# A block kernel on one core: the setup phase of the constants merged into the first attention phase

## The chip, the cores and the metric

The kernel runs on one core of a Trainium2 chip. The metric is the device time of one launch in microseconds (us), lower is better. The core has five engines that run their own instruction streams and meet at semaphores: TensorE (PE in the profile; its weight loads are PEld), VectorE (DVE), ScalarE (ACT), GpSimd (POOL) and SyncE (SP), which here only issues transfers. The granted clock of TensorE is on one of two levels, 1.2 or 2.4 GHz, and stands in the profile as a share of full speed (0.50 or 1.00). SBUF is the core's working memory of 128 partitions, PSUM (`ps`) the accumulators of TensorE.

## What is computed

Four layers on a residual stream `x` of 128 batches x 64 rows x 128 columns: cross attention, a chosen-token expert layer, a self and cross attention block with its own feed-forward part, and a mixture of experts. The outer function of the reference, and the projection part of the first layer, with which the kernel begins:

```python
    x = x + _L0_xattn_ref(_layernorm(x, axis=-1), ctx_1024, L0_xattn_Wq, ...)
    x = x + _L0_ffn_ref(_layernorm(x, axis=-1), L0_ffn_Wr, L0_ffn_Wqkv, L0_ffn_Wo)
    x = x + _L1_xattn_ref(_layernorm(x, axis=-1), ctx_1024, mask_SxS2_ik0, mask_Bx1x1xS2_if1, ...)
    x = x + _L1_ffn_ref(_layernorm(x, axis=-1), L1_ffn_router_w, ...)
...
    def _L0_xattn_ref(x, context, Wq, bq, Wk, bk, Wv, bv, Wo, bo):
        q = x @ Wq.T + bq
        k = context @ Wk.T + bk
        v = context @ Wv.T + bv
        ...
        scores = jnp.einsum('bhtd,bhcd->bhtc', q, k) / jnp.sqrt(jnp.asarray(d, x.dtype))
        attn = jax.nn.softmax(scores, axis=-1)
        out = jnp.einsum('bhtc,bhcd->bhtd', attn, v)
        ...
        return out @ Wo.T + bo
```

All of it is float32 with 16 heads of 8 columns. The mask `mask_SxS2_ik0` (64 x 64, int32) is used by the self attention of the third layer alone.

## The kernel before

The kernel is written as phases that follow one another: `setup_phase`, `attention_phase` 0 (first layer), `choice_phase` (second layer), `attention_phase` 1 and 2, `relu_phase` and `experts_phase`. Each phase is one block: the engines leave the one before through a barrier, its semaphores are cleared (`Signals.__exit__`, L56 and L57), and a jump leads into the code of the next one. Nothing of a phase starts before that.

**Constants.** All weights and small constants but the experts' lie in one array `pack` of 128 partitions x 5073 float32 (20,292 bytes a partition, 2536.5 KB). The table `COLS` gives each its columns, in the order a0, a1, a2 (643 columns for each attention phase: four weight matrices, the bias row of the output, three bias columns), ident, headmask, and the rest.

**`setup_phase` (L1926 to L1983)** loads `pack` in one transfer (L1943) and the self-attention mask in four (L1945, tile `qmi`). VectorE sets four small constants at once (L1958 to L1961), waits for `pack`, and makes from it the key biases by head group of the three attention phases (`bkm`, L1965), the scaled query bias of phase 0 (`bqs`, L1968) and a bf16 identity (`identb`, L1969). Then it waits for the mask and makes from it `qmask` and, by way of `qany`, `qdiag` and two matmuls of TensorE (L1952), `qscale` (L1971 to L1983). `bkm[1]`, `bkm[2]`, `identb`, `qmask` and `qscale` are read in attention phases 1 and 2 only.

**`attention_phase`, a = 0.** 16 groups of 512 rows. Group g+1 is prepared while the scores of group g are worked on (`pipelined`: `prep(0)`, `step(0)`, a loop of 14 steps, a last step). The preparation runs in four rounds through one PSUM bank, each a TensorE part and a copy out of PSUM by ScalarE:

- k: TensorE multiplies the context tile `ctxT` by wk (L539), ScalarE spreads it by head group into `kblk` (four ACTIVATEs, L305)
- xT: ScalarE applies the norm to `x_res` (L293), TensorE transposes (L535), ScalarE copies (L299)
- q: matmul (L541), copy (L312); v: matmuls (L544), copies (L319)

In front of xT stands the norm: statistics on VectorE (L391 to L400), `rstd` and `nmr` on GpSimd (L227, L230). A step has eight units `v`: scores (L574), maximum and shift on VectorE (L429, L431), transposes (L592), exponential on ScalarE (L338), product with v (L608); beside them run the pieces of the next group, and the end of the one before (`divide` L439 and L441, transposes L617, projection L626, residual L452).

At the phase's start SyncE issues in this order: `x_res` and `ctxT` of group 0, the same of group 1, and then two weights of the next phase, `wqkv` (1536 KB) and `woe` (512 KB); the loads of group g+2 follow when TensorE has finished the v round of group g. VectorE first fills `vblk` (L512, 128 x 4096 float32, and the two small L514 and L515), then comes to the statistics. ScalarE waits for `vblk`, and then for the first matmul.

## Time and profile before

| | us |
|---|---|
| median of 3 runs (2248.8 to 2259.13) | 2253.85 |
| the profiled execution, its own time | 2246.64 |
| span of its trace | 2244.8 |
| PE / DVE / ACT / POOL busy | 2005.9 / 1696.5 / 1060.5 / 518.5 |
| mean granted clock of TensorE | 0.959 |
| first instruction of attention phase 0 (a transfer) | 14.16 |
| first matmul of attention phase 0 | 17.70 |
| first score matmul, step 0 | 32.23 |
| end of the last instruction of attention phase 0 | 345.36 |

The 1.84 us between the span and the time lie outside the trace and are the same for both kernels here. The columns of the trace views: a timeline row is start, duration, engine, line, operation, tiles (out<-in), shape, how many were merged, and in brackets how long the engine had been idle and what ended that. PE matmuls of float32 are recorded as several passes, so one matmul of the code is two rows or more. SPq rows are transfers being issued, not landing.

### The profile page before, as it was taken

How to read it: one execution, taken by the hardware profiler on the slowest of the kernel's cores; microseconds unless marked ns; L12 is line 12 of the kernel's file. 1: busy time of each engine (PE TensorE's matmuls, PEld its weight loads, DVE VectorE, ACT ScalarE, POOL GpSimd, SP SyncE). 2: the span in 40 equal slices, each digit the busy share in tenths (PEclk: the TensorE clock that was granted, in tenths of full speed). 3: DMA queues.
4: the chain of work that ended last, by engine and by line, in shares of the span. 5: the costliest groups of instructions: out<-in, count | busy, mean ns of one | idle time of the engine just before them, and what ended most of it. 6: DMA issues, size and time to landing. Idle time of an engine off the chain costs nothing. (4 is left out here: it accounts for less than half of the span.)

```text
span 2244.8 us, 53059 instructions
## 1 busy us (share of the span) xinstructions
PE 2005.9 (89%) x19268; PEld 1549.8 (69%) x19268; DVE 1696.5 (76%) x4490; ACT 1060.5 (47%) x2084; POOL 518.5 (23%) x536
## 2 busy tenths in 40 slices
PE   5999995687769999996999997976999999999998
PEld 3666664566646666664666665755888888888887
DVE  4777775777736888885888885666888888888886
ACT  3666653455444555553555553433444444444443
POOL 1111110000001223221222222653322322232231
PEclk9999997999978999997999998997999999999999
DMA  3000000000000000001100001000000000000000
GB/s 123 29 19 27 28 10 1 1 1 0 0 1 2 0 0 0 0 0 29 30 28 28 28 10 64 0 0 1 6 11 5 5 5 10 5 5 10 5 5 10
DMA packets 27248, 30.41 MB, mean 14 GB/s; under 512 B 1936, under 2 KB 20624, under 8 KB 26896
## 3 DMA queue, kind: packets, MB, share of 16 engines
q1 hardware_dynamic: 27152, 29.28, 4.2%
q8 instruction: 42, 0.69, 0.1%
q14 instruction: 54, 0.44, 0.1%
HBM read 25.08 MB, written 4.19 MB: 13 GB/s over the span
## 5 line engine op out<-in xcount | busy, mean ns | idle before, releaser
L429 DVE TENSOR_REDUCE mx<-ps 128x8 f32<-128x512 f32 x384 | 261.9, 682 | 170.3 <-PE ps L574 169.9
L338 ACT ACTIVATE ex<-ps 128x512 f32<-128x512 f32 x384 | 230.1, 599 | 265.0 <-PE ps L592 263.2
L1111 ACT ACTIVATE moe_sg<-ps 128x512 f32<-128x512 f32 x288 | 172.5, 599 | 365.2 <-PE ps L1163 365.0
L1147 PEld LDWEIGHTS ps<-down,moe_act 128*128 128x128 f32 x2048 | 266.0, 191 | 33.0 <-DVE moe_acc L1340 12.6
L592 PE MATMUL ps<-pack,sh 128*128 128x128 f32 x1536 | 249.4, 285 | 32.1 <-DVE sh L431 31.5
L1147 PE MATMUL ps<-down,moe_act 128*128 128x128 f32 x2048 | 271.4, 275 | 5.8 <-DVE moe_acc L1340 5.8
L431 DVE TENSOR_TENSOR sh<-ps,mx 128x512 f32<-128x512 f32 x384 | 265.4, 691 | 13.2
L608 PEld LDWEIGHTS ps<-vblk,ex 128*64 128x64 f32 x6144 | 212.5, 139 | 64.6 <-issue 64.4
L608 PE MATMUL ps<-vblk,ex 128*64 128x32 f32 x6144 | 255.3, 226 | 0.0
L592 PEld LDWEIGHTS ps<-pack,sh 128*128 128x128 f32 x1536 | 168.2, 142 | 125.3 <-issue 65.2
L1322 DVE TENSOR_TENSOR moe_act<-ps,moe_sg 128x512 f32<-128x512 f32 x288 | 197.3, 685 | 68.2 <-PE ps L1163 55.6
L1340 DVE SCALAR_TENSOR_TENSOR moe_acc<-ps,moe_comb,moe_acc 128x128 f32<-128x128 f32 x768 | 215.4, 342 | 20.7 <-PE ps L1147 14.2
L574 PE MATMUL ps<-kblk,qd 32*64 32x256 f32 x3072 | 207.3, 386 | 1.5 <-issue 1.4
L1161 PE MATMUL ps<-moe_x_lo,moe_gate_hi 128*128 128x512 f32 x288 | 137.3, 477 | 26.0 <-DVE moe_act L1322 24.5
L305 ACT ACTIVATE kblk<-ps,bkm,pack 128x512 f32<-128x512 f32 x192 | 138.7, 782 | 39.2 <-PE ps L539 26.0
L574 PEld LDWEIGHTS ps<-kblk,qd 32*64 32x64 f32 x3072 | 108.5, 134 | 53.6 <-issue 8.9
L1038 POOL TENSOR_TENSOR moe_part<-moe_part 128x512 f32<-128x512 f32 x48 | 62.1, 1294 | 254.0 <-ACT moe_part L1104 254.0
L1163 PE MATMUL ps<-moe_x_hi,moe_gate_hi 128*128 128x512 f32 x288 | 114.3, 397 | 0.0
L1161 PE MATMUL ps<-moe_x_lo,moe_up_hi 128*128 128x512 f32 x288 | 114.2, 396 | 0.0
L1162 PE MATMUL ps<-moe_x_hi,moe_gate_lo 128*128 128x512 f32 x288 | 113.8, 395 | 0.0
L1163 PE MATMUL ps<-moe_x_hi,moe_up_hi 128*128 128x512 f32 x288 | 113.6, 395 | 0.0
L1162 PE MATMUL ps<-moe_x_hi,moe_up_lo 128*128 128x512 f32 x288 | 112.5, 391 | 0.0
(234 smaller groups left out, 3529.3 us busy)
## 6 DMA issues: line engine op xcount, KB each, us to landing
ctxT<-in_ctx SPq DMA_DIRECT2D x32, 256.0 KB, 2.8
x_res<-in_x SPq DMA_DIRECT2D x16, 256.0 KB, 2.9
kmi<-in_key_mask SPq DMA_DIRECT2D x16, 256.0 KB, 3.4
out<-moe_acc SPq DMA_DIRECT2D x16, 256.0 KB, 2.3
pack<-in_pack SPq DMA_DIRECT2D x1, 2536.5 KB, 9.4
wqkv<-in_wqkv SPq DMA_DIRECT2D x1, 1536.0 KB, 8.3
gate<-in_gate SPq DMA_DIRECT2D x6, 192.0 KB, 4.0
up<-in_up SPq DMA_DIRECT2D x6, 192.0 KB, 4.1
```

The costliest lines, as they stand in the source:

```text
L338: nc.scalar.activation(ex[:, u % 2], UB[u % 4].rearrange("p (c n) -> p c n", n=P), ACT.Exp).then_inc(e_ready, 1)
L429: nc.vector.tensor_reduce(mx[:, u % 2], sc, AX.X, ALU.max).then_inc(max_done, 1)
L431: nc.vector.tensor_tensor(sh[:, u % 4].rearrange("p (h k) -> p h k", k=S), sc, mx[:, u % 2].unsqueeze(2).broadcast_to((P, HH, S)), ALU.sub ...
L574: last = nc.tensor.matmul(outs[w][64 * b:64 * b + 64, t * HQ * S:(t + 1) * HQ * S], qd[rows, s, n * S:(n + 1) * S], kblk[rows, s, n].rearr ...
L592: last = nc.tensor.transpose(UB[u % 4][:, c * P:(c + 1) * P], sh[:, u % 4, c * P:(c + 1) * P], ident)
L608: last = nc.tensor.matmul(OB[m][64 * b:64 * b + 64, col:col + 32], ex[:, u % 2, c, b * S:(b + 1) * S], vblk[:, s, 2 * (2 * m + t) + b, pai ...
L1147: last = nc.tensor.matmul(YB[k % 2][:, t * D:(t + 1) * D], act_[:, k % 3, t * P:(t + 1) * P], down[:, k, :], start=True, stop=True)
L1161: nc.tensor.matmul(out, hi, y, start=True, stop=False)
L1162: nc.tensor.matmul(out, lo, x, start=False, stop=False)
L1163: return nc.tensor.matmul(out, hi, x, start=False, stop=True)
L1322: V.tensor_tensor(act_[:, k % 3], UB[k % 2], sg[:, k % 2], ALU.mult).then_inc(act_ready, 1)
L1340: last = V.scalar_tensor_tensor(acc[:, s, t], y[:, t], comb[:, s, t, k - SH:k - SH + 1], acc[:, s, t], ALU.mult, ALU.add)
```

## The change

There is no `setup_phase` any more. What it did is in `attention_phase` under `a == 0`, which takes the new argument `setup`:

- `pack` is reordered (a0, ident, headmask first: 775 columns, 387.5 KB, `FIRST`) and loaded in two transfers: the first part ahead of the loads of groups 0 and 1, the second (4298 columns, 2149 KB) behind them. The four transfers of the mask follow, then `wqkv` and `woe`.
- VectorE sets the four small constants (`first_constants`), then fills `vblk`, and then makes what phase 0 needs, `bkm[0]` and `bqs` (`loaded_constants`).
- What phases 1 and 2 need (`later_constants`) is made by VectorE at the end of step 0.
- The two matmuls for `qscale` stand in the last step at unit 2, in the PSUM bank of the preparation, and the copy of their result at unit 5.
- New waits: TensorE, GpSimd and VectorE for the first part of `pack` (`pack_loaded`), ScalarE and GpSimd for constants set (`consts_set`), VectorE for the second part and the mask (`rest_loaded`, `qmask_loaded`).

```diff
-for _n, _w in [("a0", ATTN_W), ("a1", ATTN_W), ("a2", ATTN_W), ("ident", P), ("headmask", 4),
+for _n, _w in [("a0", ATTN_W), ("ident", P), ("headmask", 4), ("a1", ATTN_W), ("a2", ATTN_W),
...
+FIRST = COLS["a1"][0]
...
             if cross:
+                if a == 0:
+                    sp.dma_start(pk[:, 0:FIRST], setup["pack_in"][:, 0:FIRST]).then_inc(pack_loaded, 16)
                 loads(0, 0)
                 loads(1, 1)
+                if a == 0:
+                    sp.dma_start(pk[:, FIRST:PACK], setup["pack_in"][:, FIRST:PACK]).then_inc(rest_loaded, 16)
+                    for r in range(4):
+                        sp.dma_start(setup["qmi"][32 * r:32 * r + 32, :, :],
+                                     setup["q_mask"].rearrange("(f r) k -> r f k", f=2)).then_inc(qmask_loaded, 16)
                 for buffer, array, loaded_ahead in ahead:
...
             def prep(g, s):
+                if a == 0:
+                    pool.wait_ge(consts_set, 1)
+                    pool.wait_ge(pack_loaded, 16)
                 inputs_of(g, s, True)
...
             act.wait_ge(vblk_set, 3)
+            if a == 0:
+                act.wait_ge(consts_set, 3)
             pipelined(act, NG, prep, step)
...
+            def first_constants():
+                nc.vector.memset(C["mhalf"][:, :], -0.5)
+                nc.vector.memset(C["half"][:, :], 0.5)
+                nc.vector.memset(C["oneb"][:, :], 1.0 / 32)
+                nc.vector.memset(setup["ones"][:, :], 1.0).then_inc(consts_set, 1)
+
+            def loaded_constants():
+                dve.wait_ge(pack_loaded, 16)
+                bias = COLS["a0"][0] + 5 * D
+                nc.vector.tensor_scalar(C["bkm"][:, 0, :], headmask, pk[:, bias + 1:bias + 2], None, ALU.mult
+                                        ).then_inc(consts_set, 1)
+                nc.vector.tensor_scalar(C["bqs"][:, :], pk[:, bias:bias + 1], SCALE, None, ALU.mult
+                                        ).then_inc(consts_set, 1)
+
+            def later_constants():
+
+                dve.wait_ge(rest_loaded, 16)
+                for n in (1, 2):
+                    bias = COLS[f"a{n}"][0] + 5 * D
+                    nc.vector.tensor_scalar(C["bkm"][:, n, :], headmask, pk[:, bias + 1:bias + 2], None, ALU.mult
+                                            ).then_inc(later_set, 1)
+                nc.vector.tensor_copy(C["identb"].rearrange("p f k -> p (f k)"), C["ident4"]).then_inc(later_set, 1)
+                dve.wait_ge(qmask_loaded, 64)
+                nc.vector.tensor_scalar(C["qmask"], setup["qmi"][:, :, :], 0.0, NEG, ALU.is_equal, ALU.mult
+                                        ).then_inc(qbias_done, 1)
...
+                    if a == 0 and not more and v == 5:
+                        dve.wait_ge(qscale_ready, 1)
+                        nc.vector.tensor_copy(C["qscale"][:, :], PREP[:, 0:S]).then_inc(qscale_copied, 1)
+                if a == 0 and first:
+                    later_constants()
                 if not more:
                     divide(g, 1)
...
+            if a == 0:
+                first_constants()
             nc.vector.memset(vblk[:, :, :, :, :], 0.0).then_inc(vblk_set, 1)
...
+            if a == 0:
+                loaded_constants()
             pipelined(dve, NG, prep, step)
...
             def prep(g, s):
+                if a == 0:
+                    pe.wait_ge(pack_loaded, 16)
                 for v in range(UNITS):
...
+                    if a == 0 and not more and v == 2:
+
+                        pe.wait_ge(qscale_diag, 2)
+                        for f in (0, 1):
+                            last = nc.tensor.matmul(PREP[:, 0:S], setup["ones"][0:32, :], setup["diag"][0:32, f, :],
+                                                    start=f == 0, stop=f == 1)
+                        last.then_inc(qscale_ready, 1)
...
-        setup_phase(nc, ps, C, pack_in, q_mask, pack, work)
```

SyncE's queue from the start of the program, before (the jump at L191 is the entry into attention phase 0) and of the change:

```order
L1943 DMA pack<-in_pack 128x5073
L1945 DMA qmi<-in_q_mask 32x2x64 x4
L1928 UNCONDITIONAL_BRANCH
L191 UNCONDITIONAL_BRANCH
L195 DMA x_res<-in_x 128x4x128
L199 DMA ctxT<-in_ctx 128x512
L195 DMA x_res<-in_x 128x4x128
L199 DMA ctxT<-in_ctx 128x512
L208 DMA wqkv<-in_wqkv 128x3072
L208 DMA woe<-in_woe 128x1024
```

```order
L219 DMA pack<-in_pack 128x775
L208 DMA x_res<-in_x 128x4x128
L212 DMA ctxT<-in_ctx 128x512
L208 DMA x_res<-in_x 128x4x128
L212 DMA ctxT<-in_ctx 128x512
L223 DMA pack<-in_pack 128x4298
L225 DMA qmi<-in_q_mask 32x2x64 x4
L228 DMA wqkv<-in_wqkv 128x3072
L228 DMA woe<-in_woe 128x1024
```

The tile `ctxT` of group 0, which the first matmul reads, moves from the sixth transfer to the third, with only the first part of `pack` ahead of it and `x_res`.

VectorE from the start of the program, before and of the change:

```order
L1961 MEMSET ones 128x128
L1965 TENSOR_SCALAR bkm<-pack 128x4 x3
L1968 TENSOR_SCALAR bqs<-pack 128x1
L1969 CAST identb<-pack 128x128
L1971 TENSOR_SCALAR qmask<-qmi 128x128
L1974 TENSOR_REDUCE qany<-qmask 128x2
L1976 TENSOR_SCALAR qany<-qany 128x2
L1980 TENSOR_SCALAR qdiag<-pack,qany 128x64 x2
L1983 COPY qscale<-ps 128x64
L1928 UNCONDITIONAL_BRANCH
L383 UNCONDITIONAL_BRANCH
L512 MEMSET vblk 128x4096
```

```order
L507 MEMSET ones 128x128
L579 MEMSET vblk 128x4096
L581 MEMSET vblk 64x128
L582 MEMSET vblk 64x128
L512 TENSOR_SCALAR bkm<-pack 128x4
L514 TENSOR_SCALAR bqs<-pack 128x1
L416 BN_STATS stats<-x_res 128x6 x4
```

The fill of `vblk` now stands directly behind the small constants and ahead of the first wait for a transfer; two small operations have come between it and the first statistics.

VectorE at the end of step 0 of the change (L464 and L466 are the `divide` of group 0, the jump at L748 leads into the loop of steps; before, that jump stood directly behind them):

```order
L464 RECIPROCAL inv<-ps 128x32
L466 TENSOR_TENSOR on<-ps,inv 128x256
L522 TENSOR_SCALAR bkm<-pack 128x4 x2
L524 CAST identb<-pack 128x128
L526 TENSOR_SCALAR qmask<-qmi 128x128
L529 TENSOR_REDUCE qany<-qmask 128x2
L531 TENSOR_SCALAR qany<-qany 128x2
L535 TENSOR_SCALAR qdiag<-pack,qany 128x64 x2
L748 UNCONDITIONAL_BRANCH
L748 ISA
L454 TENSOR_REDUCE mx<-ps 128x8
```

Eight operations have come between the `divide` and the maximum of the first unit of step 1.

TensorE in the last step of attention phase 0, of the change (L643 scores, L661 transposes, L677 product with v; before, the same row without L722):

```order
L643 MATMUL ps<-kblk,qd 64x256 x8
L661 MATMUL ps<-pack,sh 128x128 x4
L677 MATMUL ps<-vblk,ex 64x32 x8
L722 MATMUL ps<-qdiag,ones 128x64 x2
L661 MATMUL ps<-pack,sh 128x128 x4
L677 MATMUL ps<-vblk,ex 64x32 x8
```

The two matmuls for `qscale` have moved from the setup into this row, ahead of a pair of transposes and products.

## Rows read from the trace of the kernel before

**Rows 1.** Timeline, 0 to 15 us: start, duration, engine, line, what, count, [idle<-releaser].

```profile
0.74 0.40 SPq L1943 DMA_DIRECT2D pack<-in_pack  x1
...
1.19 2.16 SPq L1945 DMA_DIRECT2D qmi<-in_q_mask  x4
10.13 0.49 DVE L1965 TENSOR_SCALAR bkm<-pack 128x4 f32<-128x4 f32 x3 [8.99 <-DMA pack<-in_pack]
...
11.60 0.42 DVE L1980 TENSOR_SCALAR qdiag<-pack,qany 128x64 f32<-128x64 f32 x2
...
12.07 1.11 PE L1952 MATMUL ps<-qdiag,ones 32*128 32x64 f32 x4 [12.07 <-DVE qdiag L1980]
13.22 0.22 DVE L1983 COPY qscale<-ps 128x64 f32<-128x64 f32 x1 [1.21 <-PE ps L1952]
14.16 0.41 SPq L195 DMA_DIRECT2D x_res<-in_x  x1
14.62 0.50 SPq L199 DMA_DIRECT2D ctxT<-in_ctx  x1
```

**Rows 2.** Timeline, 15 to 31 us: the preparation of group 0 on the three engines.

```profile
15.09 3.47 DVE L512 MEMSET vblk<- 128x4096 f32 x1 [1.64 <-PEq L57]
...
17.70 2.07 PE L539 MATMUL ps<-ctxT,pack 128*128 128x512 f32 x2 [4.51 <-DMA ctxT<-in_ctx]
...
19.26 0.87 DVE L391 BATCH_NORM_STATS2 stats<-x_res 128x6 f32<-128x128 f32 x4
19.86 1.28 ACT L305 ACT_TABLE_LOAD   x1 [19.86 <-PE ps L539]
...
23.82 1.65 ACT L293 ACTIVATE xn<-x_res,nmr,rstd 128x128 f32<-128x128 f32 x4
...
30.22 2.08 PE L544 MATMUL ps<-pack,ctxT 128*128 128x128 f32 x8 [0.78 <-ACT qd L312]
```

**Rows 3.** Transfers issued at 14.62 and at 15.64: size, and us from issue to landing.

```profile
ctxT<-in_ctx SPq DMA_DIRECT2D x1, 256.0 KB, 3.0
```

```profile
ctxT<-in_ctx SPq DMA_DIRECT2D x1, 256.0 KB, 4.9
```

**Rows 4.** Stretches of 1 us: length, busy per engine, clock, DMA share, GB/s.

```profile
1.00:2.00 1.00, 0.00 (x0) 0.00 (x0) 0.14 (x2) 0.00 (x0) 0.00 (x0) 1.00 1.15 203
2.00:3.00 1.00, 0.00 (x0) 0.00 (x0) 0.00 (x0) 0.00 (x0) 0.00 (x0) 1.00 0.45 122
3.00:4.00 1.00, 0.00 (x0) 0.00 (x0) 0.00 (x0) 0.00 (x0) 0.00 (x0) 1.00 0.77 304
...
15.00:16.00 1.00, 0.00 (x0) 0.00 (x0) 0.91 (x1) 0.00 (x0) 0.00 (x0) 1.00 0.59 173
16.00:17.00 1.00, 0.00 (x0) 0.00 (x0) 1.00 (x1) 0.00 (x0) 0.00 (x0) 1.00 1.02 330
```

**Rows 5.** Timeline, 50 to 55 us: the end of step 0 and the start of step 1.

```profile
50.67 0.42 DVE L441 TENSOR_TENSOR on<-ps,inv 128x256 f32<-128x256 f32 x1
...
52.11 0.69 DVE L429 TENSOR_REDUCE mx<-ps 128x8 f32<-128x512 f32 x1 [1.01 <-PE ps L574]
...
54.38 0.60 PE L592 MATMUL ps<-pack,sh 128*128 128x128 f32 x4
```

**Rows 6.** Timeline, the last step of attention phase 0, behind its third unit.

```profile
330.17 0.66 PE L592 MATMUL ps<-pack,sh 128*128 128x128 f32 x4 [0.33 <-DVE sh L431]
```

**Rows 7.** Timeline of TensorE around 38 us, then stretches at the start of attention phase 1.

```profile
36.01 1.06 PE L592 MATMUL ps<-pack,sh 128*128 128x128 f32 x4
...
38.70 0.66 PE L592 MATMUL ps<-pack,sh 128*128 128x128 f32 x4
```

```profile
670.00:680.00 10.00, 8.48 (x70) 4.35 (x71) 5.57 (x17) 2.57 (x7) 1.22 (x2) 0.50 0.01 2
680.00:690.00 10.00, 10.00 (x80) 6.19 (x78) 2.54 (x4) 3.32 (x8) 1.27 (x1) 0.50 0.00 0
690.00:700.00 10.00, 9.66 (x134) 6.41 (x133) 6.15 (x11) 6.14 (x12) 0.00 (x0) 0.98 0.01 2
```

More of the change, by code:

```diff
@@ L64, with attention_phase @@
 HQ = 4
-def attention_phase(nc, ps, C, x_res, y_res, x_in, ctx_in, key_mask, a, ahead=()):
+def attention_phase(nc, ps, C, x_res, y_res, x_in, ctx_in, key_mask, a, ahead=(), setup=None):
     cross = a != 1
@@ L188, in attention_phase @@
         passed = sem("passed")
+        if a == 0:
+            pack_loaded = sem("pack_loaded")
+            rest_loaded = sem("rest_loaded")
+            qmask_loaded = sem("qmask_loaded")
+            consts_set = sem("consts_set")
+            later_set = sem("later_set")
+            qbias_done = sem("qbias_done")
+            qany_done = sem("qany_done")
+            qscale_diag = sem("qscale_diag")
+            qscale_ready = sem("qscale_ready")
+            qscale_copied = sem("qscale_copied")
         block = ctx.enter_context(nc.Block())
@@ L630, in prep @@
             def prep(g, s):
+                if a == 0:
+                    pe.wait_ge(pack_loaded, 16)
                 for v in range(UNITS):
@@ L1923, in _ @@
             pipelined(dve, N, prep, step)
-def setup_phase(nc, ps, C, pack_in, q_mask, pack, work):
-    with ExitStack() as ctx:
-        sem = ctx.enter_context(Signals(nc, "setup_"))
-        pack_loaded = sem("pack_loaded")
-        qmask_loaded = sem("qmask_loaded")
-        consts_set = sem("consts_set")
-        qbias_done = sem("qbias_done")
-        qany_done = sem("qany_done")
-        qscale_diag = sem("qscale_diag")
-        qscale_ready = sem("qscale_ready")
-        qscale_copied = sem("qscale_copied")
-        block = ctx.enter_context(nc.Block())
-        @block.sync
-        def _(sp):
-            sp.dma_start(pack[:, :], pack_in).then_inc(pack_loaded, 16)
-            for r in range(4):
-                sp.dma_start(work["qmi"][32 * r:32 * r + 32, :, :], q_mask.rearrange("(f r) k -> r f k", f=2)
-                             ).then_inc(qmask_loaded, 16)
-        @block.tensor
-        def _(pe):
-            pe.wait_ge(qscale_diag, 2)
-            for f in (0, 1):
-                last = nc.tensor.matmul(ps[:, 1, 0:64], work["ones"][0:32, :], work["diag"][0:32, f, :], start=f == 0,
-                                        stop=f == 1)
-            last.then_inc(qscale_ready, 1)
-        @block.vector
-        def _(dve):
-            nc.vector.memset(C["mhalf"][:, :], -0.5)
-            nc.vector.memset(C["half"][:, :], 0.5)
-            nc.vector.memset(C["oneb"][:, :], 1.0 / 32)
-            nc.vector.memset(work["ones"][:, :], 1.0).then_inc(consts_set, 1)
-            dve.wait_ge(pack_loaded, 16)
-            for a in range(3):
-                bias = COLS[f"a{a}"][0] + 5 * D
-                nc.vector.tensor_scalar(C["bkm"][:, a, :], C["headmask"], pack[:, bias + 1:bias + 2], None, ALU.mult
-                                        ).then_inc(consts_set, 1)
-            bias = COLS["a0"][0] + 5 * D
-            nc.vector.tensor_scalar(C["bqs"][:, :], pack[:, bias:bias + 1], SCALE, None, ALU.mult).then_inc(consts_set, 1)
-            nc.vector.tensor_copy(C["identb"].rearrange("p f k -> p (f k)"), C["ident4"]).then_inc(consts_set, 1)
-            dve.wait_ge(qmask_loaded, 64)
-            nc.vector.tensor_scalar(C["qmask"], work["qmi"][:, :, :], 0.0, NEG, ALU.is_equal, ALU.mult
-                                    ).then_inc(qbias_done, 1)
-            dve.wait_ge(qbias_done, 1)
-            nc.vector.tensor_reduce(work["any"][:, 0:2], C["qmask"], AX.X, ALU.max).then_inc(qany_done, 1)
-            dve.wait_ge(qany_done, 1)
-            nc.vector.tensor_scalar(work["any"][:, 2:4], work["any"][:, 0:2], 0.0, SCALE, ALU.is_equal, ALU.mult
-                                    ).then_inc(qany_done, 1)
-            dve.wait_ge(qany_done, 2)
-            for f in (0, 1):
-                nc.vector.tensor_scalar(work["diag"][:, f, :], C["ident4"][:, S * f:S * f + S],
-                                        work["any"][:, 2 + f:3 + f], None, ALU.mult).then_inc(qscale_diag, 1)
-            dve.wait_ge(qscale_ready, 1)
-            nc.vector.tensor_copy(C["qscale"][:, :], ps[:, 1, 0:64]).then_inc(qscale_copied, 1)
@@ L2004, in build @@
         C["qscale"] = sb("qscale", [P, S])
-        work = {"qmi": sb("qmi", [P, 2, S], I32), "ones": sb("ones", [P, P]), "any": sb("qany", [P, 4]),
+        setup = {"pack_in": pack_in, "q_mask": q_mask, "qmi": sb("qmi", [P, 2, S], I32), "ones": sb("ones", [P, P]), "any": sb("qany", [P, 4]),
                 "diag": sb("qdiag", [P, 2, S])}
-        setup_phase(nc, ps, C, pack_in, q_mask, pack, work)
         with ExitStack() as early:
@@ L2013, in build @@
             attention_phase(nc, ps, C, x_res, None, x_in, ctx_in, key_mask, 0,
-                            [(wqkv[:, :, :], wqkv_in, chosen_w_loaded), (woe[:, :, :], woe_in, chosen_w_loaded)])
+                            [(wqkv[:, :, :], wqkv_in, chosen_w_loaded), (woe[:, :, :], woe_in, chosen_w_loaded)], setup)
             choice_phase(nc, ps, C, x_res, wqkv, woe, chosen_w_loaded)
```

9 lines of the change are left out of this document (added).

## Prediction

> **What bounds the kernel now.** I read the timeline first, because the change touches only the first 52 us, one step at the end of attention phase 0, and nothing that later phases do. In the setup every engine waits for one transfer: `pack` is issued at 0.74 and VectorE's first operation on it starts at 10.13, after 8.99 us of idling; a short chain VectorE, TensorE, VectorE follows and ends at 13.44 (13.22 + 0.22), and the first transfer of attention phase 0 is issued at 14.16 [rows 1]. The reader is to see that nothing of phase 0 is under way by then. The second thing to see is which of three strands leads into phase 0. TensorE's first matmul waits for the context tile, starts at 17.70 and takes 2.07; ScalarE was idle up to its end (19.86) and from there works without a gap: table load 1.28, four spreads, the norm from 23.82. VectorE's strand (fill of `vblk` at 15.09, statistics at 19.26) ends earlier than it is needed [rows 2]. So the start of phase 0 goes by the landing of `ctxT`, and the whole later program goes by the start of phase 0: each phase begins behind a barrier, and what is saved ahead of 17.70 arrives at the end whole, unless something takes it back.
>
> **The gain at the start.** In the changed kernel the issue of the first part of `pack` takes the place of the issue at 0.74. The issues of `pack`, the mask and the pair at 14.16 and 14.62 stand about 0.46 us apart [rows 1], so `ctxT` of group 0 is issued at 0.74 + 2 x 0.46 = 1.66. Its landing took 3.0 us when only `x_res` was ahead of it [rows 3]. If the part of `pack` cost nothing, it lands at 4.66. It is 397 kB (775 x 4 x 128), and the engines of the queue do not start at full rate: in the first stretches after the issue of `pack` they moved 203, 122 and 304 GB/s [rows 4], which is 325 kB by 3.0 and 397 kB by 3.24. Behind it come `x_res` and `ctxT`, 524 kB. At the 330 GB/s of the second stretch after 15 us that is 1.59 us, up to 4.83. In the trace 173 + 330 = 503 of these 524 kB were through at 17.0 [rows 4], the last at about 17.06, and the landing is at 17.62: 0.56 us behind. So I put the landing at 4.83 + 0.56 = 5.4 and the first matmul, 0.08 later as before, at 5.5. **The start moves by 17.70 - 5.5 = 12.2 us.** The ends: landing at 4.66 gives 13.0; if the part of `pack` is drawn at 122 GB/s from 1.75 on, it is through at 5.0 and `ctxT` lands at 7.15, which gives 10.5.
>
> The row on which this could fail is the rate of the first 3 us, since it is that of large rows of 20 kB, of which one `pack` row now has 3.1 kB. Against the split speaks the Trainium skill, DMA: Bandwidth & Descriptors, Bandwidth and Rules for kernel authors: a transfer under 1 MiB stays below three quarters of the peak rate, and each has about 2 us fixed beside its bytes. By its formula (2.0 us and bytes over 436 GB/s, given there for transfers issued from GpSimd), taken once for three transfers that overlap, an estimate is 0.74 + 2.0 + 2.1 = 4.85 for the landing and 12.8 us for the term; were the fixed part paid three times in a row, it would be 8.9 and 8.7 us. The overlap in this trace is that of the pair at 14.16, which agrees with the first reading.
>
> Do the other strands keep up? VectorE begins at about the time of SyncE's 0.74; four small fills, the fill of `vblk` and its two small ones take 4.17 (19.26 - 15.09 [rows 2]) from about 1.2, to 5.4; `bkm[0]` and `bqs` cost a third of 0.49 each at most [rows 1], so the statistics start at 5.7, 13.5 earlier than before, where TensorE is 12.2 earlier. The part of `pack` that they wait for has landed by 3.24 + 0.56 = 3.8, under the fill. ScalarE needs `consts_set` at the end of the matmul, 7.6: set at 5.7. GpSimd's new waits are over by then too. The norm had 4.56 us from statistics to 23.82 and was not late; it now has 5.9. So ScalarE stays the strand as it was, table load included, at no cost.
>
> **Queue of SyncE.** It now issues twelve transfers in a row; the second part of `pack` and the mask stand behind the loads of groups 0 and 1 and in front of `wqkv` and `woe`. Group 1's context took 4.9 us from issue when 1.8 MB of weights came behind it [rows 3]; with 0.5 us of issue each and 0.8 us of `pack` ahead it lands at about 8.5. Its reader stands inside step 0, whose first scores move from 32.23 (table above) to 20.0: cover 11.5 us or more. All that is queued, 5.8 MB, needs 17.6 us at 330 GB/s from 1.75 on, to 19.4; the loads of group 2 are issued when the v round of group 0 ends (30.22 + 2.08 [rows 2]), now at 20.1 or later, and are read a step later. The issues of the four mask transfers (2.16 us [rows 1]) pass only transfers of which none is urgent. Cost nought; without that cover it would be a few us of group 2's landing, still inside step 1.
>
> **What is moved into steps.** `later_constants`: before, the chain from 10.13 to 12.02 with three `bkm` and one `bqs`; without one `bkm` (0.13) and the `bqs` (0.07) it is 1.7 us. It waits for transfers that landed 20 us earlier. It stands behind the `divide` of step 0, where VectorE then idled 1.01 us until TensorE's scores [rows 5]. So 0.7 us stick out: queued behind are maximum and shift of unit 0 of step 1, for which TensorE's transposes wait. Maximum and shift, 0.69 and about as much from 52.11 on, ended at about 53.5, and the transposes ran at 54.38, because TensorE was busy [rows 5]: 0.7 more is just hidden. Ends 0 and 0.9 (none of the cover, and a loop entry behind it); I take 0.2. In the last step the two matmuls (four passes) took 1.11 us in the setup with TensorE at its lower level [rows 1]; at the upper one half, 0.55. They stand ahead of transposes before which TensorE idled 0.33 for VectorE [rows 6]. That leaves 0.2. Ends 0 and 0.8, the copy of 0.22 [rows 1] being counted in.
>
> **Sum:** 12.2 - 0.2 - 0.2 = 11.8 us. From the profiled execution: 2246.64 - 11.8 = 2234.8. That execution lies 7.2 us below the median of the three runs and below the lowest of them, so the forecast for a median is 2253.85 - 11.8 = 2242.05, some 0.5% faster.
>
> **Rivals.**
>
> *The clock in the first phase (0.2).* TensorE starts at its lower level: transposes take 1.06 us at 36.01 and 0.66 at 38.70 [rows 7], so the rise is between them, about 8 us after TensorE's dense work began at 30.22 [rows 2]. In attention phase 1 the lower level lasted 20 us of dense work, from 670 to 690 [rows 7]. There 80 passes ran in 10 us against 134 afterwards: each us at the lower level costs 0.40 us. If the rise needs 20 us after the dense start at 18.0, it takes back 12 x 0.40 = 4.8: gain 7.0, 2246.9. If it comes at once, 3.3 more are gained: 2238.8. For it speaks the spread between the two rows; against it that the work in front of step 0 has the same pattern as before. The Trainium skill, TensorE: Matmul & The Clock Gate, Part 1, says that the point of the rise differs from run to run of one kernel. By that rule the term has no sign of its own.
>
> *The first landing is late (0.15).* The split does not do what it says: the queue serves the third transfer not in turn but together with the 2149 KB behind it. The 4.9 us of the tile that had large weights behind it [rows 3], from 1.66, with 0.9 for `pack`: 7.5 to 8; with the slow first stretches up to 10. Gain 10 to 7.5: 2244 to 2246.4. Against it: at 17.62 the tile landed on time although the loads of group 1 were issued right behind it (15.64 [rows 3]).
>
> *The exposed constants (in the forecast's range).* 1.7 us for both moved pieces in full: 2243.3.
>
> *Slower (0.06).* Lower-level stretches at the starts of all phases. Their length goes by where a phase's start falls, and every start moves by 12 us. The stretch shown costs up to 20 x 0.40 = 8 us [rows 7]. To end over 2265 the five later and first starts together must lose 23 us against the forecast, 58 us more at the lower level. Decided where the sum of these stretches grows by over 30 us (gain gone) and 58 us (slower). Nothing in the change pushes that way; it could as well shrink.
>
> **How the numbers follow.** Forecast 0.59, clock 0.2 (a quarter of it on the early side), landing 0.15, slower 0.06. The predicted time is 2242. The terms' ends give 13.0 down to 10.5 - 1.7 = 8.8 at the start and in the steps, 2240.9 to 2245.1, with the clock 2237 to 2250. Runs of one kernel here differ by 10 us, and the profiled one is below all three, which draws the low end down: 2233 to 2251. A measurement can tell about 0.5%, 11.3 us, from no change; the forecast of 11.8 lies on that bound. So of the forecast's 0.59 I give 0.34 to faster, of the clock's 0.06 and of the landing's 0.03; with runs that come out low 0.03 more. Faster 0.46, within 0.5% 0.48, slower 0.06.
>
> **What the profile will show.** First matmul at 5.5 (5 to 7), with the wait on `ctxT`, not on `pack`. Statistics at 5.7. Norm on ScalarE directly behind the spreads at about 11.6. Step 0's first scores at 20.0. DMA busy up to about 19 without a gap. Maximum of step 1 at 40.6 with no idle ahead of it, and the transposes behind it 14 to 12 us earlier than 54.38. End of phase 0 at 333.6 instead of 345.4. I am wrong if the first matmul starts later than 7.5, if ScalarE waits for VectorE or GpSimd in the preparation of group 0, if the rise of the clock comes over 12 us after the dense start, or if later phases differ by over 3 us in length.

## The result, and the profile after

The changed kernel takes 2243.22 us (median of 20 runs, 2237.82 to 2255.73), the kernel before in the same comparison 2252.07 us (20 runs, 2247.54 to 2266.58). The ratio is 0.9956, with a 95% interval of 0.9944 to 0.9969: a gain of 9.9 us, 7.0 to 12.6. In a later comparison, told below, the change came out at 0.9936 (0.9914 to 0.9959), 14.5 us (9.3 to 19.4). The prediction said 11.8 us and 2242, and gave a chance of 0.48 to a time within 0.5% of before, which the measured 0.44% is, and 0.46 to a larger gain. That the time came within 1.2 us of the forecast is in part luck: the gain is 1.9 us smaller (2.9 by the medians, which differ by 8.85), and the kernel before came out 1.8 us lower than the 2253.85 that the forecast starts from.

The profiled execution of the change took 2248.79 us (span 2246.7), more than the profiled one before (2246.64, span 2244.8). Read alone, that pair of traces says that nothing was won. Its timeline shows otherwise at the start, columns as in [rows 1]:

```profile
0.75 0.40 SPq L219 DMA_DIRECT2D pack<-in_pack  x1
...
1.68 0.50 SPq L212 DMA_DIRECT2D ctxT<-in_ctx  x1
1.95 3.47 DVE L579 MEMSET vblk<- 128x4096 f32 x1 [0.80 <-issue]
...
5.96 2.04 PE L608 MATMUL ps<-ctxT,pack 128*128 128x512 f32 x2 [5.96 <-DMA ctxT<-in_ctx]
...
6.31 0.86 DVE L416 BATCH_NORM_STATS2 stats<-x_res 128x6 f32<-128x128 f32 x4
...
8.11 1.28 ACT L328 ACT_TABLE_LOAD   x1 [8.11 <-PE ps L608]
9.40 2.79 ACT L328 ACTIVATE kblk<-ps,bkm,pack 128x512 f32<-128x512 f32 x4
...
12.08 1.65 ACT L316 ACTIVATE xn<-x_res,nmr,rstd 128x128 f32<-128x128 f32 x4
...
20.50 1.13 PE L643 MATMUL ps<-kblk,qd 32*64 32x256 f32 x8
```

The first matmul stands at 5.96 against 17.70 and waits for `ctxT` as before; ScalarE works through from 8.11 as it did from 19.86 [rows 2]; the first scores are at 20.50 against 32.23. 11.74 us are there. Then TensorE's transposes and scores of step 0:

```profile
38.15 1.06 PE L661 MATMUL ps<-pack,sh 128*128 128x128 f32 x4
...
40.14 1.99 PE L643 MATMUL ps<-kblk,qd 32*64 32x256 f32 x16
...
47.82 1.09 PE L643 MATMUL ps<-kblk,qd 32*64 32x256 f32 x16
48.84 0.66 PE L661 MATMUL ps<-pack,sh 128*128 128x128 f32 x4
```

They take 1.06 and 1.99 us until 46, and 0.66 and 1.09 from 47.8 on. Before, the same fall from 1.06 to 0.66 lay between 36.01 and 38.70, some 6 us behind the first scores [rows 7]; here it lies 27 us behind them. The reciprocal that ends step 0 comes 24.32 us behind the first scores instead of 18.07, and of 11.74 us won 2.55 are left at the phase's end. Whether the change does that is the question for the experiments.

### The profile page after: what moved, and what is told of

It reads as the page before. It is cut to its first block and busy times, and to the rows that moved or that the text cites. A ratio compares the mean times of both kernels' runs of the same rounds, so it can differ in the third digit from the quotient of the medians.

```text
span 2246.7 us, 53038 instructions
## 1 busy us (share of the span) xinstructions
PE 2018.1 (90%) x19268; PEld 1558.3 (69%) x19268; DVE 1698.7 (76%) x4490; ACT 1064.3 (47%) x2084; POOL 518.5 (23%) x536
## 5 line engine op out<-in xcount | busy, mean ns | idle before, releaser
L661 PE MATMUL ps<-pack,sh 128*128 128x128 f32 x1536 | 252.8, 287 | 31.5 <-DVE sh L456 30.9
L677 PEld LDWEIGHTS ps<-vblk,ex 128*64 128x64 f32 x6144 | 214.3, 139 | 66.0 <-issue 66.0
L661 PEld LDWEIGHTS ps<-pack,sh 128*128 128x128 f32 x1536 | 170.4, 143 | 126.2 <-issue 66.6
L677 PE MATMUL ps<-vblk,ex 128*64 128x32 f32 x6144 | 257.3, 227 | 0.0
L1418 DVE SCALAR_TENSOR_TENSOR moe_acc<-ps,moe_comb,moe_acc 128x128 f32<-128x128 f32 x768 | 216.4, 345 | 20.3 <-issue 11.1
L643 PE MATMUL ps<-kblk,qd 32*64 32x256 f32 x3072 | 209.4, 389 | 1.4 <-issue 1.4
L643 PEld LDWEIGHTS ps<-kblk,qd 32*64 32x64 f32 x3072 | 109.1, 135 | 54.4 <-issue 10.0
## 6 DMA issues: line engine op xcount, KB each, us to landing
wqkv<-in_wqkv SPq DMA_DIRECT2D x1, 1536.0 KB, 11.1
```

Source lines behind the costliest of these rows:

```text
L643: last = nc.tensor.matmul(outs[w][64 * b:64 * b + 64, t * HQ * S:(t + 1) * HQ * S], qd[rows, s, n * S:(n + 1) * S], kblk[rows, s, n].rearr ...
L661: last = nc.tensor.transpose(UB[u % 4][:, c * P:(c + 1) * P], sh[:, u % 4, c * P:(c + 1) * P], ident)
L677: last = nc.tensor.matmul(OB[m][64 * b:64 * b + 64, col:col + 32], ex[:, u % 2, c, b * S:(b + 1) * S], vblk[:, s, 2 * (2 * m + t) + b, pai ...
L1418: last = V.scalar_tensor_tensor(acc[:, s, t], y[:, t], comb[:, s, t, k - SH:k - SH + 1], acc[:, s, t], ALU.mult, ALU.add)
```

## The experiments

All use one table of milestones, in us from the start of the span (a mean where there are several traces; phase 0 ends with the last instruction of VectorE in it):

```
                                  first    first   scores to   end of    span
                                  matmul   scores  reciprocal  phase 0
before, 3 traces                  17.91    32.43   18.07       345.5     2244.8 to 2253.7
change, profiled execution         5.96    20.50   24.32       342.8     2246.7
change, 3 more traces              6.10    20.62   18.07       334.2     2234.2 to 2239.2
waits filled, before              17.75    30.52   17.08       342.5     2253.8
waits filled, change               6.01    18.21   17.10       330.8     2233.5
merged, pack whole                11.76    26.28   18.08       339.9     2243.4
pack split, setup phase kept       8.66    23.19   18.08       336.7     2239.8
filled, order and constants moved  4.69    17.79   17.09       330.3     2232.6
filled at all starts               4.79    18.71   21.14       335.1     2231.3
the same, tuned                    5.22    16.52   17.08       328.9     2220.4
```

**Both kernels looked at again.** No edit.

> The changed kernel once more, unchanged, for a second trace of its start. In the first one TensorE's clock rose about 27 us after the first scores (20.5), against 6 us in the trace of before. Theory chance (where the rise falls is drawn anew in each execution): first matmul again at 6.0, first scores at 20.5, but the rise anywhere from 24 to 48 us, and step 0 between 18.8 and 27.3 us long. Theory lasting (the change itself makes the rise late): rise again at 47 to 48 and step 0 of 27 us.

> The kernel before once more, unchanged, for a second trace. Theory chance: first matmul at 17.7 and first scores at 32.2 as in the first trace, but the rise anywhere from 36 to 60 us. Theory lasting: the rise again at 38, 6 us after the first scores, and step 0 again of 18.8 us.

The change took 2240.97 us, before 2255.48. In this trace of the change the clock rises early:

```profile
24.70 1.06 PE L661 MATMUL ps<-pack,sh 128*128 128x128 f32 x4
27.31 0.66 PE L661 MATMUL ps<-pack,sh 128*128 128x128 f32 x4 [0.41 <-DVE sh L456]
```

Phase 0 ends at 334.52 against 345.61: 11.1 us. So the late rise doesn't belong to every execution of the change.

**TensorE's waits filled, in either kernel.** Matmuls on `oneb` into a PSUM bank that nothing reads at the time stand where TensorE would wait. The result is untouched.

```diff
                 if a == 0:
+                    pe.wait_ge(consts_set, 1)
+                    keep_busy(nc, C, UB[3], 9)
                     pe.wait_ge(pack_loaded, 16)
...
+                    if a == 0 and v == slots["k"]:
+                        keep_busy(nc, C, UB[3], 12)
+                    if a == 0 and v in (slots["xT"], slots["q"]):
+                        keep_busy(nc, C, UB[3], 1)
...
+def keep_busy(nc, C, bank, n):
+    for _ in range(n):
+        nc.tensor.matmul(bank[0:64, :], C["oneb"][:, :], C["oneb"][:, :].unsqueeze(1).broadcast_to((P, 8, S)),
+                         start=True, stop=True)
```

> The changed kernel with idle waits of TensorE in the preparation of group 0 filled with matmuls whose result nobody reads (9 of 512 columns in bf16 before the first real one, 12 behind the k round, one each behind xT and q). Both theories: the clock is at its upper level when step 0 begins (20.5 or up to 1.5 earlier), step 0 takes 17.5 to 19 us. Chance: before loses some 2 to 5 us to the lower level in step 0 on average and the changed kernel as much, so this run is 14 to 17 us under before. Lasting: the changed kernel loses 8.6 us each time, so this run is 18 to 20 us under before, 8 to 9 under the changed kernel. This trace also shows the moved constants at full clock: VectorE's idle time of 1.01 us ahead of step 1 gone, and the transposes behind it late by 0 to 0.9 us.

> The kernel before with the same filling: 24 such matmuls while the setup waits for the constants, 7 before the first matmul of phase 0, and 12, 1 and 1 in the preparation. Its step 0 runs at the upper level too, so the difference to the filled changed kernel is free of the clock's place: 11.5 us (11.7 less 0.2 for the moved constants) by both theories. Against the kernel before: 2 to 5 us faster by chance, under 1 us by lasting (there the kernel before has its early rise each time).

The change with filling: 2237.41 us, ratio to before 0.9927 (0.9906 to 0.9948). Before with filling: 2255.45, ratio 0.9996 (0.9973 to 1.0018). TensorE in the preparation of the filled change:

```profile
7.99 3.99 PE L751 MATMUL ps<-oneb 128*64 128x512 bf16 x12
...
15.22 1.12 PE L610 MATMUL ps<-srcT,pack 128*128 128x512 f32 x2 [0.34 <-ACT srcT L322]
16.28 0.40 PE L751 MATMUL ps<-oneb 128*64 128x512 bf16 x1
17.12 1.16 PE L613 MATMUL ps<-pack,ctxT 128*128 128x128 f32 x8 [0.44 <-ACT qd L335]
```

The q and v rounds take 1.12 and 1.16 us, where the unfilled ones took 2.08 each. In either kernel some 3 us are won by the end of phase 0 (345.5 to 342.5, 334.2 to 330.8), and the difference between the filled kernels there is 11.7 us (12.3 at the first scores). So the start's gain doesn't hang on the level of the clock. The two times don't decide between the two theories: the filled change lies 16.4 us under before (11.7 to 21.2), inside the 14 to 17 of *chance*; the filled kernel before lies 0.9 us under it (4.1 above to 6.1 under), where *chance* had 2 to 5 and *lasting* under 1. The 3 us that its trace shows at the end of phase 0 are 0.13%, inside that interval. In this trace they were lost again at the start of attention phase 2, as told below, and something of the kind seems the rule: the mean granted clock of its ten executions is 0.947 to 0.956 (median 0.952), that of the kernel before on the same chip 0.953 to 0.960 (0.958), although its phase 0 runs more at the upper level. Why, no run shows.

**One half of the change at a time.** First the merged phase with `pack` in one transfer ahead of the loads:

```diff
-                    sp.dma_start(pk[:, 0:FIRST], setup["pack_in"][:, 0:FIRST]).then_inc(pack_loaded, 16)
+                    sp.dma_start(pk[:, :], setup["pack_in"]).then_inc(pack_loaded, 16)
                 loads(0, 0)
                 loads(1, 1)
...
-                    sp.dma_start(pk[:, FIRST:PACK], setup["pack_in"][:, FIRST:PACK]).then_inc(rest_loaded, 16)
```

Then the change with a phase of its own, and so with the barrier, for the first part of `pack`, the four small constants, `bkm[0]` and `bqs`; the loads of groups 0 and 1 and all else follow behind it:

```diff
+        early_phase(nc, C, setup)
...
+def early_phase(nc, C, setup):
...
+            sp.dma_start(pk[:, 0:FIRST], setup["pack_in"][:, 0:FIRST]).then_inc(pack_loaded, 16)
...
-            if a == 0:
-                first_constants()
...
-            if a == 0:
-                loaded_constants()
```

> The changed kernel, but all of the constants in one transfer at the head of the queue (no split, no reordering in time), all else as in the change. Theory parts (merging the phases and splitting the load each give about half): the large transfer lands at 10, the context behind it at 11.2, the first matmul at 11.3 instead of 6.0 and the first scores at 25.8. Rival (the merging is all that counts, the queue serves transfers together): first matmul at 7 to 8. The end of phase 0 goes by the clock's rise as well; it is read from the first matmul and the first scores.

> The reverse: a small setup phase with its barrier is kept, but loads only the first part of the constants and makes the key bias and query bias of phase 0; the rest of the load, the mask and the later constants are in phase 0 as in the change. Theory parts: constants landed at 4.0, small operations to 4.5, barrier and jump 0.7, first load of phase 0 issued at 5.2, first matmul 3.5 later at 8.7, first scores at 23.3; so the barrier is worth 2.7 of the 11.7 us. Rival (merging is what counts): first matmul at 12 or later.

They took 2245.5 and 2241.64 us (one execution each), before on that chip 2258.52. Both first matmuls came near what the theory of parts has (11.76 and 8.66, expected 11.3 and 8.7). By the first scores merging alone gains 6.2 us, the split with its barrier kept 9.2, both 11.8: doing away with the phase of its own is worth 2.6 once the load is split, and the split 5.7 once the phases are merged; the other 3.5 come with either. The second kernel also has the mask and the later constants moved into phase 0, and its trace shows what that is worth (of its start, the landing told by the first operation on `pack`):

```profile
3.93 0.23 DVE L1995 TENSOR_SCALAR bkm<-pack 128x4 f32<-128x4 f32 x1 [2.79 <-DMA pack<-in_pack]
4.06 0.15 DVE L1997 TENSOR_SCALAR bqs<-pack 128x1 f32<-128x1 f32 x1
4.89 0.42 SPq L206 DMA_DIRECT2D x_res<-in_x  x1
```

From the first operation on `pack` to the first load of phase 0 it is 0.96 us, before 14.16 - 10.13 = 4.03 [rows 1]. So of its 9.2 us some 6.2 are the earlier landing (10.13 to 3.93), and 3.1 the shorter chain of small operations behind it.

With `pack` whole in front, the loads behind it don't get through earlier (timeline of the first kernel, then its first transfers with KB and us from issue to landing, a median where there are two):

```profile
2.92 4.25 SPq L211 DMA_DIRECT2D ctxT<-in_ctx  x1
...
10.05 0.23 DVE L510 TENSOR_SCALAR bkm<-pack 128x4 f32<-128x4 f32 x1 [3.98 <-DMA pack<-in_pack]
...
11.76 2.05 PE L605 MATMUL ps<-ctxT,pack 128*128 128x512 f32 x2 [11.76 <-DMA ctxT<-in_ctx]
```

```profile
pack<-in_pack SPq DMA_DIRECT2D x1, 2536.5 KB, 9.3
x_res<-in_x SPq DMA_DIRECT2D x2, 256.0 KB, 10.0
ctxT<-in_ctx SPq DMA_DIRECT2D x2, 256.0 KB, 10.1
```

**Context first, constants later.** The filled change with `ctxT` ahead of the first part of `pack`, and `later_constants` at unit 3 of step 0 (and with 7 instead of 9 unread matmuls ahead of the first one):

```diff
                 if a == 0:
+                    sp.dma_start(ctxT[:, 0], ctx_in[:, 0:TOK]).then_inc(c_loaded[0], 16)
                     sp.dma_start(pk[:, 0:FIRST], setup["pack_in"][:, 0:FIRST]).then_inc(pack_loaded, 16)
...
+                    if a == 0 and first and v == 3:
+                        later_constants()
...
-                if a == 0 and first:
-                    later_constants()
```

> The filled changed kernel with two edits: the context of group 0 is issued ahead of the first part of the constants, and these ahead of its rows; and the moved constants stand at unit 3 of step 0, where VectorE idles 1.5 us, instead of behind the divide. If the first matmul goes by the bytes ahead of its last input, it starts at 5.2 (650 kB instead of 921). From the reciprocal at the end of step 0 to the maximum of step 1 it is 2.23 us in the filled changed kernel and 1.67 in the kernels without moved constants: 1.67 here if the constants cost 0.5 us by their place, 2.23 if the loop entry makes it. First scores at 17.5, end of phase 0 at 329.5 (330.8 in the filled changed kernel).

2234.68 us (one execution). The order gives 1.3 us at the first matmul (4.69 against 6.01; in the two kernels below, with the same order, it starts at 4.79 and 5.22), and ScalarE, which now waits for the last of VectorE's constants, begins 1.7 us earlier (6.49 against 8.16) and comes to the norm as much earlier (10.44 against 12.13):

```profile
6.49 1.28 ACT L332 ACT_TABLE_LOAD   x1 [6.49 <-DVE bqs L518]
...
10.44 1.65 ACT L320 ACTIVATE xn<-x_res,nmr,rstd 128x128 f32<-128x128 f32 x4
```

Only 0.4 of it reach the first scores (17.79; expected 17.5). In this trace the filling ended at 8.96, TensorE waited 3.28 us for the norm, and the q round took 2.07 us again. In the tuned kernel below, with four more matmuls there, it takes 1.13 and the first scores stand at 16.52, the whole 1.7 earlier than 18.21. The constants: the maximum of step 1 comes 1.66 us behind the reciprocal (before 1.66 to 1.82, change 2.23), so their place makes the 0.5 us there. Yet little of it reaches the end of the phase, 295.4 us behind the reciprocal (330.3, expected 329.5): it is 295.2 and 295.3 in the two kernels below, 295.4 to 295.6 in the kernels with the constants behind the `divide`.

**Filling at the later starts too.** Matmuls of the same kind at the starts of the choice phase, of attention phases 1 and 2, of the relu phase and (in the first of the two kernels alone) of the experts phase. The second kernel has 16 instead of 12 behind the k round of group 0.

```diff
...
+                else:
+                    keep_busy(nc, C, UB[3], 24 if a == 1 else 12)
...
+                    if a == 1 and v == slots["k"]:
+                        keep_busy(nc, C, UB[3], 8)
+                    if a == 2 and v == slots["k"]:
+                        keep_busy(nc, C, UB[3], 6)
...
+            keep_busy(nc, C, HB[3], 12)
```

> The same, and TensorE's idle waits at the start of all later phases filled too (24 and 8 unread matmuls in attention phase 1, 12 and 6 in phase 2, 14, 18 and 4 in the choice phase, 12 ahead of the relu phase, 20, 2, 3 and 30 in the experts phase). If the lower-level stretches of 20 to 41 us behind each phase start are paid for at 0.40 us each, about 35 us of dense work at the lower level are saved, some 12 to 16 us; with the 16 of the filled changed kernel and 1.3 of the two edits it ends 28 to 34 us under the kernel before. Rival (the filling delays as much as it saves, or the clock falls all the same at the barriers): 16 to 20 us under the kernel before.

> The change, with unread matmuls in TensorE's waits at the starts of attention phases 0, 1, 2 and of the choice phase (16 instead of 12 behind the k round of group 0, none in the experts phase), the context tile ahead of the first part of pack, and the later constants at unit 3 of step 0. Nothing of the computation is left out. Theory (a wait at a phase's start that is filled keeps or brings the upper clock, and the filling in the experts phase cost 4 us): span 2227 to 2229, median 2229, ratio to before 0.989. Rival (the filling only shifts where the clock falls, and what the run before this gained in the attention phases is chance): span as in the run with filling in phase 0 alone, 2232.6, median 2235, ratio 0.992.

The first took 2233.46 us, ratio 0.9889 (0.9856 to 0.9921), the second **2229.57 us**, ratio 0.9881 (0.9856 to 0.9906). On the chip of the second the change as it is had 2242.53 and 0.9936 (0.9914 to 0.9959): the intervals don't meet, 13.0 us lie between the medians. Those 13.0 us are filling and reordered loads together; no run parts them. The first kernel lies 25.1 us under before (17.8 to 32.5), less than the 28 to 34 expected and more than its rival's 16 to 20; the second came out as expected by its time, while its trace, of the fastest of its five executions, is shorter than expected (2220.4 against 2227 to 2229). Lengths of the phases, from the end of phase 0 on:

```
                             choice  attention 1  attention 2  relu   experts
before                       304.3   384.1        345.2        133.8  732.1
before, again                307.0   384.3        350.5        133.8  732.4
before, third                304.8   384.3        350.6        133.8  732.1
change                       306.9   385.0        346.1        134.4  731.5
change, 3 more               306.2   384.5        346.1        134.0  732.4
before, phase 0 filled       304.0   384.3        356.1        133.3  733.5
filled at all starts         300.8   381.5        343.1        134.5  736.3
the same, tuned              300.3   381.4        343.1        134.6  732.1
```

Against the change filling wins some 4 to 7 us in the choice phase (which takes 304.4 to 307.3 in the single traces of the change), 3 in attention phase 1 and 3 in attention phase 2, nothing in the relu phase, and lost 4 in the experts phase. Attention phase 2 also shows what makes traces of one kernel differ: its first stretch at the lower level lasted 30.7, 41.0 and 54.6 us where it took 345.2, 350.5 and 356.1 (granted clock 0.50 from 1021.5 to 1052.2 in the first of these). Filling doesn't hold the upper level by itself. In the first of these two kernels the transposes of step 0 went to 0.66, back to 1.11 and to 0.66 again, and the step took 21.14 us instead of 17.1:

```profile
24.20 0.66 PE L665 MATMUL ps<-pack,sh 128*128 128x128 f32 x4 [1.22 <-DVE sh L460]
25.52 1.11 PE L665 MATMUL ps<-pack,sh 128*128 128x128 f32 x4
...
34.44 1.06 PE L665 MATMUL ps<-pack,sh 128*128 128x128 f32 x4
37.09 0.66 PE L665 MATMUL ps<-pack,sh 128*128 128x128 f32 x4
```

Since one kernel had 12 and the other 16 matmuls in the long wait, and one trace each, whether the four more or chance kept the second from it is open.

**How often is the rise late?** No edit, three more traces.

> The change as it is, timed again in five rounds beside the kernel above, and a third trace of it. If the late rise of the clock in the profiled execution (27 us after the first scores, 8.6 us lost) is a rare event of single executions, this trace shows the rise about 6 us after the first scores (reciprocal of step 0 18.1 us behind the first scores), end of phase 0 near 334.6, span about 2239, median about 2242. If the change makes it late as a rule, the reciprocal comes 21 to 25 us behind the first scores and the end of phase 0 near 340 to 343.

> The kernel before, a third trace. If the late rise does not hang on the change, it may show here too, with about the same chance as in the change; the two traces of it so far rise early (18.07 us from first scores to reciprocal in both). Early: 18.1 us, end of phase 0 near 345.4. Late: 21 us or more, end of phase 0 at 348 or later.

> The change as it is, a fourth trace, for the same question: early rise as in the second trace (reciprocal of step 0 18.1 us behind the first scores, end of phase 0 near 334.6, span 2238 to 2241), or late as in the first (24.3 us, 342.8).

2242.53 us (median of 6 runs), 2252.95 and 2236.31 (one execution each). All three rise early (18.07 us from scores to reciprocal), with phase 0 ending at 334.19, 345.55 and 333.88. Over the nine traces of kernels without filling, one is late: the profiled execution of the change. It cost 342.81 - 334.2 = 8.6 us there. One late rise among four traces of the change and none among three of the kernel before can't tell whether the change makes it likelier.

## Why the prediction was right, point by point

**The start (12.2 us) was the whole effect; it measured 11.8.** First matmul at 6.10 in the mean of three traces and 5.96 in the fourth, expected 5.5 (5 to 7), waiting on `ctxT`. Stretches of 1 us from 1.0 to 6.0 in the profiled execution, columns as in [rows 4]:

```profile
1.00:2.00 1.00, 0.00 (x0) 0.00 (x0) 0.20 (x3) 0.00 (x0) 0.00 (x0) 1.00 0.45 50
2.00:3.00 1.00, 0.00 (x0) 0.00 (x0) 1.00 (x1) 0.00 (x0) 0.00 (x0) 1.00 0.62 214
3.00:4.00 1.00, 0.00 (x0) 0.00 (x0) 1.00 (x1) 0.00 (x0) 0.00 (x0) 1.00 1.03 345
4.00:5.00 1.00, 0.00 (x0) 0.00 (x0) 1.00 (x1) 0.00 (x0) 0.00 (x0) 1.00 1.07 371
5.00:6.00 1.00, 0.04 (x1) 0.07 (x1) 0.67 (x3) 0.00 (x0) 0.00 (x0) 1.00 1.10 323
```

The working let 921 kB pass (first part of `pack`, `x_res`, `ctxT`) up to 4.83 and the tile land 0.56 later. The bytes were right by two errors that cancel: 264 kB at 3.0 instead of 325, then 345 and 371 GB/s instead of 304 and 330, and 921 kB were through at 4.84. But the tile landed at 5.78 (issue 1.68 and the 4.1 below), when 1232 kB had passed. The term mis-sized is the lag behind the bytes, 0.94 instead of 0.56. Of the 1232 kB 311 belong to later transfers, the first of them group 1's tiles, issued at 2.22 and 2.69, which were served in between; that they are what makes the lag longer is likely and not shown. It would be the mechanism of the rival *the first landing is late*, at 0.4 us instead of the 1.8 to 4.3 that it was given.

```profile
pack<-in_pack SPq DMA_DIRECT2D x1, 387.5 KB, 3.2
...
ctxT<-in_ctx SPq DMA_DIRECT2D x1, 256.0 KB, 4.1
```

The estimate by the Trainium skill's formula (DMA: Bandwidth & Descriptors, Anatomy of one DMA) was 4.85 with the fixed part once and 8.9 with it three times; 5.78 measured is 0.9 above the first and 3.1 under the second.

**The other strands kept up.** `vblk` began at 1.95, not 1.2 (0.80 of "issue" ahead of it), and the statistics at 6.31, not 5.7; it cost nothing, ScalarE came to the norm at 12.08 directly behind its spreads. The queue of SyncE was free of harm: group 1's context landed 5.8 us after its issue at 2.69, long before its reader, and `woe`, the last, at 18.8 (6.51 and 12.3). (The weights behind the tile of the 4.9 us were 2.1 MB, 1536 and 512 KB, and not the 1.8 MB of the working; nothing else rests on it.)

**Constants moved into step 0: 0.2 predicted, at most 0.4 measured.** The second look at the change, VectorE and TensorE around the `divide`, and then the reciprocal in the kernel before:

```profile
38.99 0.35 DVE L464 RECIPROCAL inv<-ps 128x32 f32<-128x32 f32 x1
39.38 0.42 DVE L466 TENSOR_TENSOR on<-ps,inv 128x256 f32<-128x256 f32 x1
...
39.72 0.35 DVE L522 TENSOR_SCALAR bkm<-pack 128x4 f32<-128x4 f32 x2
...
40.89 0.42 DVE L535 TENSOR_SCALAR qdiag<-pack,qany 128x64 f32<-128x64 f32 x2
41.22 0.69 DVE L454 TENSOR_REDUCE mx<-ps 128x8 f32<-128x512 f32 x1
...
43.08 0.60 PE L661 MATMUL ps<-pack,sh 128*128 128x128 f32 x4
```

```profile
50.30 0.35 DVE L439 RECIPROCAL inv<-ps 128x32 f32<-128x32 f32 x1
```

The maximum has no idle ahead of it, as foreseen, and is about 0.5 us late. The transposes stand 43.08 - 38.99 = 4.09 us behind the reciprocal, before 54.38 - 50.30 = 4.08 [rows 5]: hidden at this place. Undoing the move won at most 0.4 us by the end of the phase (295.2 to 295.4 from the reciprocal to it instead of 295.4 to 295.6), no more than traces differ.

**Matmuls in the last step: 0.2 predicted, 0.19 measured.** From the same look, and then a row of the kernel before:

```profile
318.14 0.66 PE L677 MATMUL ps<-vblk,ex 128*64 128x32 f32 x16
...
318.73 0.65 PE L722 MATMUL ps<-qdiag,ones 32*128 32x64 f32 x4
...
319.32 0.66 PE L661 MATMUL ps<-pack,sh 128*128 128x128 f32 x4
```

```profile
329.18 0.66 PE L608 MATMUL ps<-vblk,ex 128*64 128x32 f32 x16
```

From product to transposes it is 1.18 us; before, 0.99 (329.18 to 330.17 [rows 6]).

**Sum.** At the end of phase 0 the early traces of the two kernels differ by 345.5 - 334.2 = 11.3 us, 11.8 expected. Of the 0.5 between 11.8 at the first scores and 11.3, the last step is 0.19; the other 0.3 accrue between step 0's end and the last step, and no run explains them, though the moved constants may be a part. Behind phase 0 two things are left. The time outside the span is not the same for both kernels, as the text ahead of the prediction has it: 1.8 us in the three traced executions of the kernel before and 2.1 in the four of the change (2248.79 - 2246.7), 0.2 to 0.3 that the change loses. And 11.3 at the end of phase 0 became 9.9 us of device time in one comparison and 14.5 in the other, with 11.3 inside both intervals. A late rise in some executions would pull the gain down (8.6 us in one execution of four would be 2.2 on the mean, an estimate), but how often it comes is not known.

**Rivals.** *The clock in the first phase* is real: one traced execution in four lost 8.6 us by it, where the prediction had at most 4.8. The price of 0.40 us for each us at the lower level holds (27 - 6 = 21 us more, 8.4 by it); the length was mis-sized, since the row of attention phase 1 gave 12 us more. It differs between executions of one kernel, and is not shown to hang on the change. The prediction's own sign of error, a rise over 12 us after the dense start, occurred in the profiled execution. The Trainium skill (TensorE: Matmul & The Clock Gate, Part 1) has the upper level come soon once work is sustained; this trace doesn't agree: scores still take 1.99 us at 40.14, after 20 us in which TensorE never waited. *Slower by the later starts* didn't happen: from the end of phase 0 to the end of the trace it is 1899 to 1908 us before and 1900 to 1905 after. The sign given for it, later phases that differ by over 3 us, says little: in the profiled pair they differ by 4.4 in all (1903.9 against 1899.5), and two traces of the kernel before by 8.6.

## What to carry to other kernels

At a program's start, order the queue by who reads first: a first part of 387.5 KB in front of the tile that the first matmul needs, and the bulk behind, was worth 5.7 us here once the phases were merged, and doing away with a phase of its own for the constants 2.6 once the load was split. What isn't needed yet (here the mask and the later constants) is best taken out of the chain ahead of the first load: 3.1 us in the split kernel. Price a start by the milestones of its phase in several traces, and not by the span of one pair: here the pair differed by 1.9 us to the wrong side, though each lay within its kernel's spread. Where an engine's wait at a phase's start can't be shortened, matmuls that nobody reads can be laid into TensorE's idle time; here that gave, together with the reordered loads, 13 us more. It has to be measured over the whole program: in the first phase of the kernel before alone it won 3 us there and nothing that the time shows, and in the experts phase it lost 4.

## What the runs showed of the hardware

- The upper level of TensorE's clock can stay out for 27 us of dense work (transposes 1.06 us until 46), in a program whose other traces have it after 6. After filled waits it was there at 24.20, gone at 25.52 and back at 37.09, within one step. The Trainium skill (TensorE: Matmul & The Clock Gate, HAM oscillation) tells of the clock falling in waits for transfers; the fall ahead of 25.52 came in step 0, where its longest wait was 1.22 us, and the tuned kernel had the same wait without a fall.
- A transfer of 2536.5 KB in front of 256 KB tiles held these until it was through (landing 9.7 to 10.4 us after issue, against 3.0 [rows 3]), and SyncE stood 4.25 us in the issue of the fourth tile behind it, 0.51 in the change.
- From 1.0 to 3.0 the queue moved 50 and 214 GB/s with the first part of `pack` in front (rows of 3.1 kB) and 203 and 122 with the whole of it (rows of 20 kB) [rows 4]; from 3.0 to 4.0 it was 345 and 304. That the length of the rows makes the difference is not shown: the transfers behind differ too. The clock column reads 1.00 in these stretches, though the first matmuls show the lower level: where TensorE hasn't worked yet, it says nothing.
